# Output biases of the chosen experts: gathered rows added by VectorE, or a product on TensorE

## The reference

```
gates  = softmax(xf @ gate_w + gate_b)              # 16 experts
topv, topi = top_k(gates, 2);  combine[n, e] = the gate of a chosen expert, else 0
routed = sum_e combine[n, e] * (gelu(xf @ ew1[e] + eb1[e]) @ ew2[e] + eb2[e])
shared = sum_s gelu(xf @ sw1[s] + sb1[s]) @ sw2[s] + sum_s sb2[s]     # 2 shared experts, width 2048
out    = x + shared + routed                        # xf: the normalised x
```

## Time and profile before

| | |
|---|---|
| median of 3 runs | 870.17 us |
| the profiled execution | 869.57 us |
| its span | 867.9 us |
| TensorE busy | 844.7 us |
| VectorE busy | 597.1 us |
| ScalarE busy | 472.3 us |
| GpSimd busy | 193.7 us |
| granted TensorE clock | full (1.0) throughout |

### The profile page before, as it was taken

One profiled execution on the slowest core, in us unless ns is written; L12 is line 12 of the kernel. 1 busy time (PEld: TensorE's weight loads), 2 busy tenths in 40 slices (PEclk: granted clock), 3 DMA queues, 4 the chain that ended last, 5 costly groups with the idle time before them and its releaser, 6 DMA issues.

```text
span 867.9 us, 14451 instructions
## 1 busy us (share of the span) xinstructions
PE 844.7 (97%) x4150; PEld 701.5 (81%) x4150; DVE 597.1 (69%) x1276; ACT 472.3 (54%) x843; POOL 193.7 (22%) x232
## 2 busy tenths in 40 slices
PE   3899999999999999999999999999999999999998
PEld 2668888888888888888888888888888889998886
DVE  7987889966687778555787786555677544443784
ACT  6678766454476563454656464445456256555541
POOL 3110000021100000112000001111121488754880
PEclk9999999999999999999999999999999999999999
DMA  8904644387343333574433324655698388868986
GB/s 222 292 24 120 170 124 121 98 165 137 96 139 98 97 98 100 125 175 86 146 118 99 98 74 102 113 121 161 174 205 202 102 258 280 265 210 275 306 251 196
DMA packets 127405, 135.45 MB, mean 156 GB/s; under 512 B 10520, under 2 KB 88912, under 8 KB 126828
## 3 DMA queue, kind: packets, MB, share of 16 engines
q1 hardware_dynamic: 117612, 108.47, 46.9%
q0 software_dynamic: 8784, 25.11, 9.7%
q10 hardware_dynamic: 944, 1.07, 0.5%
HBM read 111.63 MB, written 22.98 MB: 155 GB/s over the span
## 4 chain that ended last, share of the span: by engine, by line
PE 95%; ACT 1%; DMA 1%; DVE 1%; SPq 1%; issue 0%; POOL 0%; DVEq 0%; POOLq 0%; ACTq 0%
PE up L639 13%; PE up L641 13%; PE up L640 13%; PE acc L700 13%; PE acc L702 13%; PE acc L705 13%; PE up L891 5%; PE up L809 2%; PE acc L639 1%; PE acc L641 1%; PE acc L640 1%; PE up L665 1%; PE acc L817 1%; PE misc L665 1%; PE misc L724 1%; DMA vin<-in_ctx 1%
## 5 line engine op out<-in xcount | busy, mean ns | idle before, releaser
L639 PE MATMUL up<-xs,w1hi 128*128 128x512 f32 (+1 forms) x512 | 198.9, 388 | 0.0
L641 PE MATMUL up<-xs,w1lo 128*128 128x512 f32 (+1 forms) x512 | 195.9, 383 | 0.0
L640 PE MATMUL up<-xs,w1hi 128*128 128x512 f32 (+1 forms) x512 | 195.4, 382 | 0.0
L700 PE MATMUL acc<-w2hi,hhi 128*128 128x512 f32 x486 | 189.6, 390 | 0.0
L702 PE MATMUL acc<-w2lo,hhi 128*128 128x512 f32 x486 | 189.2, 389 | 0.0
L969 ACT ACTIVATE hhi<-up,b_col 128x512 fp32r<-128x512 f32 x128 | 86.5, 676 | 157.3 <-PE up L641 113.4
L1246 DVE TENSOR_TENSOR hlo<-hf,hhi 128x512 fp32r<-128x512 f32 x128 | 85.8, 670 | 74.0 <-ACT hf L972 30.4
L705 PE MATMUL acc<-w2hi,hlo 128*128 128x512 f32 x486 | 130.8, 389 | 0.0
L641 PEld LDWEIGHTS up<-xs,w1lo 128*128 128x128 f32 x512 | 96.2, 188 | 19.2
L639 PEld LDWEIGHTS up<-xs,w1hi 128*128 128x128 f32 x512 | 96.2, 188 | 18.7 <-issue 0.5
L640 PEld LDWEIGHTS up<-xs,w1hi 128*128 128x128 f32 x512 | 96.3, 188 | 18.1
(11 more groups left out here) (284 smaller groups left out, 1085.7 us busy)
## 6 DMA issues: line engine op xcount, KB each, us to landing
w_raw<-in_L_ffn_sw SPq DMA_DIRECT2D x256, 256.0 KB
expert_rows<-ysb SPq DMA_DIRECT2D x47, 256.0 KB
xn_rows<-kn POOLq DMA_DIRECT2D x16, 256.0 KB
e2raw<-in_L_ffn_ew SPq DMA_DIRECT2D x16, 256.0 KB, 6.1
ew_sb<-in_L_ffn_ew SPq DMA_DIRECT2D x16, 256.0 KB
X<-in_x SPq DMA_DIRECT2D x12, 256.0 KB, 7.7
vin<-in_ctx SPq DMA_DIRECT2D x12, 256.0 KB
out<-X SPq DMA_DIRECT2D x12, 256.0 KB
```

The costliest lines, as they stand in the source:

```text
L639: nc.tensor.matmul(o, lhs[0], rhs[0], start=start, stop=False)
L640: nc.tensor.matmul(o, lhs[0], rhs[1], start=False, stop=False)
L641: return nc.tensor.matmul(o, lhs[1], rhs[0], start=False, stop=stop)
L700: nc.tensor.matmul(acc[t][:], hh, w2hi[:, slot], start=first and (q > 0 or t >= HT) or again, stop=False)
```

## The change

`cb96`, `cbT`, `bias_f`, `bias_r`, their loads, casts, transposes and products go. `route_pick` also writes the two chosen experts as integers (`bias_at`). GpSimd gathers, for each of the 128 tokens of a tile, the eb2 rows of its two experts from DRAM into `bias_g` (two gathers of 256 KB), after `store_rows` of j = 0 and before the tile's scatter. VectorE adds them to the tile's rows `X2` with the gates behind `route_place` (j = 2), and the sum of the two sb2 rows (`bias_s`, made once) with a third pass. `take_block` waits for the down products themselves. `lgT`, the copy of the gate logits, gets a buffer of its own.

```diff
@@ SyncE
-            sp.wait_ge(con.sem, con.at(0, "bias0"))
-            for r in range(3):
-                sp.dma_start(bias_f[32 * r:32 * r + E], eb2).then_inc(c_in, 16)
-                sp.dma_start(bias_f[32 * r + E:32 * r + E + S_EXP], sb2).then_inc(c_in, 16)
             for p in range(PRE):
                 load_pre(p)
+            sp.wait_ge(tz, 16)
+            for e, row in ((0, bias_s[:]), (1, bias_g[:, 0])):
+                sp.dma_start(row, sb2[e:e + 1].broadcast_to([P, D])).then_inc(s_in, 16)
@@ TensorE
-                    if isinstance(c, int) and n == CH - 1:
-                        pe.wait_ge(con.sem, con.at(0))
-                        pe.wait_ge(bias_hi, 3)
-                        pe.wait_ge(cbt_ok, TB * (q + 1))
-                        for t in range(TB):
-                            last = nc.tensor.matmul(acc[t][:], cbT[:, t], bias_r[:], start=False, stop=True)
-                        last.then_inc(acc_ready, 1)
...
             def routing_products(t):
-                pe.wait_ge(rt.sem, rt.at(t, "lo"))
-                nc.tensor.transpose(misc[0:BR, CBT0:CBT0 + P], cb96[:], ident[:])
+                pe.wait_ge(rt.sem, rt.at(t, "mem"))
...
-                nc.tensor.matmul(acc[t][:], cbT[:, t], bias_r[:], start=False, stop=True).then_inc(tile_ready, 1)
+                last.then_inc(tile_ready, 1)
@@ ScalarE
-            def combine_T(t, tb, q):
-                act.wait_ge(rank_ps, t + 1)
-                need(act, acc_ready, q)
-                nc.scalar.copy(cbT[:, tb], misc[0:BR, CBT0:CBT0 + P]).then_inc(cbt_ok, 1)
...
-            for at in (0, 32, 64):
-                nc.scalar.copy(bias_r[at:at + 32], bias_f[at:at + 32]).then_inc(bias_hi, 1)
@@ VectorE
+                rdo(V.tensor_copy(bias_at[:], idxf[:]))
...
-                rdo(V.tensor_scalar(comb2[:], oh[:, 0], top8[:, 0:1], None, ALU.mult))
-            def route_combine(t):
...
             def route_place(t):
                 dve.wait_ge(rank_ps, t + 1)
-                dve.wait_ge(cbt_ok, t + 1)
...
+            def route_bias(q, tb, t):
+                rows = X2[:, q, tb]
+                dve.wait_ge(bias_in, 32 * (t + 1))
+                for j in range(2):
+                    if j:
+                        after(rt, t, "bias0")
+                    rdo(V.scalar_tensor_tensor(out=rows, in0=bias_g[:, j], scalar=top8[:, j:j + 1], in1=rows,
+                                               op0=ALU.mult, op1=ALU.add))
+                after(con, 0, "shb")
+                after(rt, t, "bias1")
+                rdo(V.tensor_tensor(rows, rows, bias_s[:], ALU.add))
...
             def take_block(q):
-                dve.wait_ge(acc_ready, q + 1)
+                dve.wait_ge(down_done, CH * (q + 1))
+                after(rt, TB * (q + 1) - 1, "bias2")
...
                     if j == 1:
-                        route_combine(t)
...
                     if j == 2:
                         route_place(t)
+                        route_bias(q, tb, t)
@@ GpSimd
+            def gather_bias(t):
+                pool.wait_ge(rt.sem, rt.at(t, "bi"))
...
+                for j in range(2):
+                    pool.indirect_dma_start(out=bias_g[:, j], out_offset=None, in_=eb2[:, :],
+                                            in_offset=bass.IndirectOffsetOnAxis(ap=bias_at[:, j:j + 1], axis=0))\
+                        .then_inc(bias_in, 16)
...
                     if j == 0 and q < NQ - 1:
                         store_rows(TB * (q + 1) + tb, xt)
+                    if j == 0:
+                        gather_bias(TB * q + tb)
                     if j == 2:
                         scatter(TB * q + tb)
```

More of the change, by code:

```diff
@@ L224, in mixed_layer @@
         trow_i = sb("trow_i", [P, 1], i32)
-        zero_i = sb("zero_i", [P, (TROWS * P) // P], i32)
+        zero_mem = ExitStack()
+        zero_i = sb("zero_i", [P, (TROWS * P) // P], i32, zero_mem)
+        zero_mem.close()
+        bias_s = sb("bias_s", [P, D])
         wkv_mem = ExitStack()
@@ L356, in mixed_layer @@
         gsm = Steps(sem("gsm"), "parts lg max sub sum rec gates")
-        rt = Steps(sem("rt"), "gt max idx idxf c e o1 o2 mem wc comb hi h0 h1 lo rank m1 m2 pos pint pall msum")
-        con = Steps(sem("con"), "keep0 keep1 first0 boost0 cap shift c0 c1 half bias0 ms ones o16 cb0 cb1 cb2 gz qz pz ghi glo blo")
+        rt = Steps(sem("rt"), "gt max idx idxf c e bi o1 o2 mem rank m1 m2 pos pint pall msum bias0 bias1 bias2")
+        con = Steps(sem("con"), "keep0 keep1 first0 boost0 cap shift c0 c1 half ms ones o16 gz qz pz ghi glo shb")
         pcon = Steps(sem("pcon"), "ramp id0 tri0 sel0 id tri sela selb ie eb thr ip tok stage z")
@@ L703, in __new__ @@
                     need(pe, h_lo, c + 1)
+                    ends = isinstance(c, int) and n == CH - 1
                     for t in tiles:
@@ L706, in __new__ @@
                                                 start=False,
-                                                stop=isinstance(c, int) and c == HOLD - 1 and acc[t] in y_bank)
+                                                stop=ends or isinstance(c, int) and c == HOLD - 1
+                                                and acc[t] in y_bank)
                     last.then_inc(down_done, 1)
@@ L847, in tile @@
                         pe.wait_ge(gsm.sem, gsm.at(q, "lg"))
-                        pe.wait_ge(cbt_ok, t)
-                        pe.wait_ge(rt.sem, t * len(rt.names))
+                        if not isinstance(t, int) or t:
+                            pe.wait_ge(rt.sem, rt.at(t - 1, "rank"))
                         transpose_x(t + TB, xt, misc)
@@ L936, in _ @@
                     nc.tensor.matmul(acc[t][:], hhi[:, slot, tok], w2lo[:, slot], start=False, stop=False)
-                    nc.tensor.matmul(acc[t][:], hlo[:, slot, tok], w2hi[:, slot], start=False, stop=False)
-                nc.tensor.matmul(acc[t][:], cbT[:, t], bias_r[:], start=False, stop=True).then_inc(tile_ready, 1)
+                    last = nc.tensor.matmul(acc[t][:], hlo[:, slot, tok], w2hi[:, slot], start=False,
+                                            stop=c == NCH - 1)
+                last.then_inc(tile_ready, 1)
         @block.scalar
@@ L1572, in route_pick @@
                 rdo(V.tensor_tensor(member[:], oh[:, 0], oh[:, 1], ALU.add))
-                rdo(V.tensor_scalar(comb2[:], oh[:, 0], top8[:, 0:1], None, ALU.mult))
-            def route_combine(t):
-                after(rt, t, "wc")
-                rdo(V.scalar_tensor_tensor(out=comb[:], in0=oh[:, 1], scalar=top8[:, 1:2], in1=comb2[:],
-                                           op0=ALU.mult, op1=ALU.add))
-                after(rt, t, "comb")
-                rdo(V.tensor_copy(chi[:], comb[:]))
-                after(rt, t, "hi")
-                rdo(V.tensor_copy(cb96[:, 0:E], f(chi[:])))
-                rdo(V.tensor_copy(cb96[:, 32:32 + E], f(chi[:])))
-                rdo(V.tensor_tensor(cb96[:, 64:64 + E], comb[:], f(chi[:]), ALU.subtract))
             def route_place(t):
                 dve.wait_ge(rank_ps, t + 1)
-                dve.wait_ge(cbt_ok, t + 1)
                 rdo(V.tensor_tensor(rb[:], misc[:, RANK0:RANK0 + E], ebase[:], ALU.add))
@@ L1626, in _ @@
             const(V.memset(ones16[:], 1.0))
-            const(V.memset(cb96[:], 0.0))
-            after(con, 0, "cb0")
-            const(V.memset(cb96[:, E:E + S_EXP], 1.0))
-            const(V.memset(cb96[:, 32 + E:32 + E + S_EXP], 1.0))
             const(V.memset(f(gw2[:]), 0.0))
@@ L1702, in _ @@
             split_w1(2, 2)
-            bias_low()
+            shared_bias()
             for q in range(NQ):
```

43 lines of the change are left out of this document (16 added, 27 removed).

## The result

| kernel | median us | against the kernel before (interval of 95%) |
|---|---|---|
| before, beside the change | 870.20 (14 runs) | 1 |
| changed | 871.63 (14 runs) | 1.0018 (1.0010 to 1.0026) |
| changed, measured again | 873.94 (6 runs) | 1.0062 (1.0042 to 1.0083) |

What follows compares the result with a forecast made beforehand. TensorE was taken as the bound, other engines mattering only where they hand over late. Terms -5.4 (TensorE) + 0.8 (last quad) + 0.1 (block changes) = -4.5, from the median 870.17 to 865.7 us; 8-in-10 range 864.0 to 870.2.

Steps and rivals of the forecast that it cites:

- TensorE's part: TensorE loses bias products and gate-matrix transposes, all on the path: -5.4 us, ends -5.4 and -7.7.
- Products: The 16 bias products on TensorE go, 0.23 us each: 3.7 us.
- Transposes: The 16 gate-matrix transposes on TensorE go: 1.7 us by start distance, up to 4.0 with the gap behind each group.
- VectorE's own work: Three passes per tile, less what goes: net +1.7 us ahead of the next low halves, 16 times, VectorE far from the bound.
- the landing L: Time from a gather pair's issue to its use by VectorE: taken as 6.5 us, from gathers of expert rows.
- w: VectorE's wait per tile for its gathers: 2.0 us in block 0's tile 1, 0 in blocks 1 and 2.
- the room of 4.3: Block 0, tile 1: how late VectorE's low half of w2 may be before TensorE waits, 6.0 us less 1.7.
- rival 2: Gathers queue behind scatters and stores, last quad loses most: 877.0 us at a landing of 10; chance 0.14 slower, 0.12 within 0.2%.
- Last quad: Tiles 13 to 15: VectorE waits for gathers, TensorE stalls 0.25 and 0.55 us, then none: +0.8 us.
- Block changes: VectorE frees the accumulators later while TensorE comes sooner; covered by only 0.3 us, put at +0.1 us.
- rival 3: VectorE's lateness makes additions at block changes late: 2.4 us lost with waits of 1.5 at two changes, 868.1; chance 0.06.
- Start: Start phase: removed loads and casts and earlier weights gain 0, within 0.5 us.

Runs made afterwards that it cites:

- e10: The kernel before without its 16 bias products, transposes, copies and casts kept (no output biases); 865.21 us, ratio 0.9960.
- e5: The changed kernel with neither VectorE's bias passes nor the gathers (no output biases of the experts); 863.13 us, ratio 0.9936.
- e1: The changed kernel with the three passes per tile on rows loaded once, no gathers issued or waited for; 864.79 us, ratio 0.9953.
- e6: The changed kernel with block 2's context rows (1 MB) loaded six chunks earlier; 868.25 us, ratio 0.9989.
- e15: e6 with each of block 0's eight table scatters replaced by a transfer of one element; 867.50 us, ratio 0.9981.
- e14: e6 with a tile's pair of gathers issued ahead of the row store instead of behind it; 868.12 us, ratio 0.9994.
- e2: The changed kernel with the same gathers and passes, but the passes read bias_s and do not wait for the gathers; 869.82 us, ratio 1.0001.
- e11: e2 with the context rows loaded earlier; 864.01 us, ratio 0.9935.
- e13: The changed kernel itself, unaltered, measured again; 873.94 us, 4.7 us over the kernel before.
- e7: The changed kernel with block 0's passes one step later and, in the last quad, two gather buffers and passes behind the next pick; 866.06 us, ratio 0.9963.
- e8: e7 with the context rows loaded earlier, the whole computation; 863.77 us, ratio 0.9935.

## Why the prediction was wrong, step by step

- **TensorE's part was right in kind and low in size.** Products: 3.7 expected, 3.9 measured (e10). Transposes: I took 0.107 each from the start distance; by the marks they cost 0.165, 2.6 in all for 1.7 (2.2 by the medians). By the marks 1.60 per block is 6.4 us, by e5's median 6.1, for 5.4 in the prediction: inside its ends of 5.4 and 7.7.
- **VectorE's own work** (+1.7 us a tile, no stall) held in blocks 1 and 2 and, within 0.3 us, in the last quad; in block 0 it cost 1.8 (e1), where weights are late.
- **The step that failed is the landing L in block 0's tile 1.** I took 6.5 us, from gathers that have no scatter ahead of them; it is 12.6 and 13.1 in two traces. The rest of the chain stands: its w was L - 4.5, so 8.1 with the true L (7.22 measured, the issue being 1.3 us sooner); less the room of 4.3 that leaves 2.9 of the measured wait for TensorE, which stood for 3.4. The prediction even had the evidence, the store's 13.7 us and the scatter's landing of over 10 us, but used it only for a guess of "about 1 more in block 0" inside rival 2, and gave no weight to the context rows issued in the same microseconds. e6 shows that they make 3.4 of the 12.6, e15 that the scatters make at least 3.9 more, e14 that the store's place ahead of the pair makes none of it (behind the pair it is still in flight beside it).
- **A second cost in the same place was not seen at all:** the gathers make weights late even where nobody waits for the gathers (e2: 4.7 us idle; e11: gone). In the changed kernel the two are not additive: a w2 is 20.6 us under way there too, and no gap follows it. That the late weight alone makes a stall is shown by e2; that the wait alone does is the sum above (7.22 for 4.3), without a run of its own.
- **The clock behind a stall** was not in the sum. It makes most of the nearly 2 us that block 0 loses beyond its gap.
- **Last quad:** mechanism and place right. Waits of 1.15, 2.05 and 2.65 expected, 1.78, 0.59 and 2.55 measured, landings of 5.6, 4.3 and 5.7. Stalls 0.8 expected, 1.7 measured, 2.5 by the marks. But L moves from one execution to the next: 6.2, 4.9 and 8.0 in e13, where the quad loses 7.3. Rival 2's place and its price in L hold there; its loss of 5.4 us, reckoned for L = 8.1 in every tile, is passed already with these landings: with e13's waits of 2.31, 1.20 and 4.85 the gaps are 1.63, 0.61 and 2.83, 5.1 in all, and the wider starts and the lower clock behind them bring the rest.
- **Block changes** and rival 3: in both traces of the changed kernel block 1 takes its 179.66, without a late addition; right. Only the margin of 0.3 us was not there: with a wait of 1.00 in tile 3 e7 loses 0.94, and with one of 0.29 e14 still loses 0.26.
- **Start:** the first gate product at 71.59 for 71.72; right.
- Sum of the misses, from 865.7 to the first trace: block 0 +5.3, last quad +1.7, tail +1.7, products and transposes -1.0, block changes -0.1, the routed stage -0.8 (124.77 for 125.52), the profiled execution's distance from the median of before -0.6: 871.9, and that execution took 871.87.

That a transfer behind scatters comes late was a rule which I had cited for rival 2 (the Trainium skill, DMA: Bandwidth & Descriptors, Queues, rings and completion order: a transfer's mark lands behind every earlier write of its DMA engine, across its queues; the page writes it of the queues of SyncE and ScalarE). e15 agrees with it in effect, 5.3 for 9.2 us once the scatters are away, and the w2 loads of the other queue with 2.8 for 9.0. So a place behind the scatters in GpSimd's own queue is not the whole cause. But the records of q1 last longer as well, so that it need not be the marks alone that come late; what the scatters do inside the DMA engines stays open, no run separated it.

## What to carry to other kernels

Price a new transfer from a row in the same stretch of the program, behind the same neighbours: the landings of the other transfers there tell best whether the DMA engines are free, their share comes next, and their GB/s mislead. Where an engine must wait in order for a gather, put the use one or two steps behind the issue and give it a second buffer; e8 did no less work than the changed kernel and got 0.9 of the possible gain. And move a large load that isn't urgent out of the stretch that the new traffic uses, even if it costs nothing where it is.

## What was not expected of the hardware

- Beside two scatters of 128 elements of 4 bytes a load of 256 KB in another queue takes 9.0 us to land in the median, beside two single elements 2.8; the share of the DMA engines is 0.96 at 60 GB/s over 5 us, for 0.53 at 164 GB/s. The Trainium skill (DMA: Bandwidth & Descriptors, Specifications) says that below 512 bytes a piece an engine reads, modifies and writes; the runs agree that such pieces are dear, and show nothing of the way.
- In that stretch 256 KB of weights took 20.6 us to land from the end of the issue (e2), and a pair of 256 KB gathers 12.6; with scatters and context rows away, under 5.3.
- A pause of 3.4 us of TensorE is followed by products 0.43 us apart for 0.23; after one of 2.8 us (e13), and after one of 1.97 us too (e6, last quad), the granted clock of the next five microseconds is 0.66.
- The same kernel measured twice differs by 2.3 us in the median where its traces differ in the last quad alone by 4.8: late gathers make a kernel's time less steady, and e8's five runs lie within 1.6 us.
